# A two-layer token mixer on one core: the hand-written order of its calls on four engines is replaced by another order of the same calls

## The reference

```
x = x + layernorm(attn(layernorm(x)))
x = x + layernorm(ffn(layernorm(x)))

attn(h): conv = causal convolution of h over the sequence, kernel C * sigmoid(A)**t * B, plus D * h
         z = gelu(conv) @ W_proj.T + b_proj
         return layernorm(h + z) * gamma + beta
ffn(h):  r = sigmoid((mu_r*h + (1-mu_r)*h_prev) @ W_r.T)
         k = relu((mu_k*h + (1-mu_k)*h_prev) @ W_k.T) ** 2
         return r * (k @ W_v.T)
```

## Time and profile before

| What | Value |
|---|---|
| median of 3 runs | 150.51 us (150.22 to 150.79) |
| the profiled execution's own time | 150.25 us |
| its span, first to last instruction | 148.5 us |
| PE busy | 135.5 us (91%) |
| DVE, ACT, POOL busy | 130.8, 129.6, 127.5 us (88%, 87%, 86%) |
| DMA moved | 8.99 MB |
| chain that ended last | PE 73%, POOL 17%, DVE 4% |

### The profile page before, as it was taken

One profiled execution on the slowest core, in us unless ns is written; L12 is line 12 of the kernel. 1 busy time (PEld: TensorE's weight loads), 2 busy tenths in 40 slices (PEclk: granted clock), 3 DMA queues, 4 the chain that ended last, 5 costly groups with the idle time before them and its releaser, 6 DMA issues.

```text
span 148.5 us, 3239 instructions
## 1 busy us (share of the span) xinstructions
PE 135.5 (91%) x950; PEld 116.0 (78%) x950; DVE 130.8 (88%) x372; ACT 129.6 (87%) x388; POOL 127.5 (86%) x176
## 2 busy tenths in 40 slices
PE   6778888989999999999999999999999999999910
PEld 6667787876988799797979797988887887777900
DVE  0989999999999988999997999998999899339981
ACT  4878999799699999979779999959998988999940
POOL 4599999998989988989896998978999899978282
PEclk9999999999999999999999999999999999999995
DMA  3999900000000002000200002200200200424524
GB/s 89 235 328 272 299 22 0 0 2 0 0 4 0 0 0 77 0 2 0 75 0 0 0 4 71 73 0 7 71 2 0 71 4 0 141 68 138 152 72 141
DMA packets 18705, 8.99 MB, mean 61 GB/s; under 512 B 1536, under 2 KB 18688, under 8 KB 18688
## 3 DMA queue, kind: packets, MB, share of 16 engines
q1 hardware_dynamic: 17840, 8.52, 19.7%
q10 hardware_dynamic: 848, 0.26, 0.7%
HBM read 4.59 MB, written 4.19 MB: 59 GB/s over the span
## 4 chain that ended last, share of the span: by engine, by line
PE 73%; POOL 17%; DVE 4%; DMA 2%; issue 1%; POOLq 1%; ACT 0%
PE ps_k L855 9%; PE ps_k L856 9%; PE ps_r L867 9%; PE ps_r L866 9%; PE ps_tv L876 9%; PE ps_z L833 7%; POOL x_r L227 5%; POOL xn_pow L236 5%; PE ps_tv L846 5%; PE ps_prefix L813 4%; PE ps_z L834 4%; PE ps_xT L805 3%; PE ps_prefix L819 2%; PE ps_prefix L815 2%; DMA a_col<-in_A_param 2%
## 5 line engine op out<-in xcount | busy, mean ns | idle before, releaser
L370 ACT ACTIVATE xn<-x_all,x_bias,x_r 128x128 f32<-128x128 f32 x64 | 26.4, 499 | 1.1 <-POOL x_bias L218 0.6
L867 PE MATMUL ps_r<-mixed_T,tsT 128*128 128x128 f32 x128 | 24.7, 275 | 0.0
L866 PE MATMUL ps_r<-mixed_T,tsT 128*128 128x128 f32 x128 | 24.7, 275 | 0.0
L833 PE MATMUL ps_z<-pv_T,gelu 128*128 128x128 f32 x128 | 22.1, 275 | 0.0
L426 ACT ACTIVATE f_normal<-f,out_bias,yf_r 128x128 f32<-128x128 f32 x48 | 19.8, 493 | 1.5 <-POOL out_bias L285 1.5
L236 POOL TENSOR_TENSOR xn_pow<-xn,pow_token 128x512 f32<-128x512 f32 x16 | 20.3, 1273 | 0.0
L866 PEld LDWEIGHTS ps_r<-mixed_T,tsT 128*128 128x128 f32 x128 | 19.5, 192 | 0.5 <-issue 0.5
L833 PEld LDWEIGHTS ps_z<-pv_T,gelu 128*128 128x128 f32 x128 | 19.4, 191 | 0.5 <-issue 0.5
L389 ACT ACTIVATE junk<-ps_z 128x128 f32<-128x128 f32 x64 | 16.7, 280 | 3.2 <-PE ps_z L834 3.2
L867 PEld LDWEIGHTS ps_r<-mixed_T,tsT 128*128 128x128 f32 x128 | 19.4, 192 | 0.0
L834 PE MATMUL ps_z<-ident,xnT 128*128 128x128 f32 x64 | 17.4, 273 | 0.0
(11 more groups left out here) (112 smaller groups left out, 360.1 us busy)
## 6 DMA issues: line engine op xcount, KB each, us to landing
out_x<-x_all SPq DMA_DIRECT2D x15, 256.0 KB, 2.2
x_all<-in_x SPq DMA_DIRECT2D x7, 512.0 KB, 6.0
x_all<-in_x SPq DMA_DIRECT2D x2, 128.0 KB, 2.8
x_all<-in_x SPq DMA_DIRECT2D x1, 256.0 KB, 3.2
out_x<-x_all SPq DMA_DIRECT2D x1, 128.0 KB, 1.8
out_x<-x_all ACTq DMA_DIRECT2D x1, 128.0 KB, 1.9
w_pv<-in_W_proj ACTq DMA_DIRECT2D x1, 64.0 KB, 2.6
w_pv<-in_W_v ACTq DMA_DIRECT2D x1, 64.0 KB, 4.5
```

Source lines behind the costliest of these rows:

```text
L370: last = a_.activation(tile(xn[u % D], j), xa(u, j), ACT.Identity, bias=col(x_bias, u, j), scale=col(x_r, u, j))
L833: t_.matmul(tile(ps_z[u % 3], j), tile(gelu[u % D], j), pv_T[:, 0, :], start=True, stop=False)
L866: t_.matmul(tile(ps_r, j), tsT[u % D][:, q, l + 1:l + 1 + P], mixed_T[:, 0, :], start=True, stop=False)
L867: last = t_.matmul(tile(ps_r, j), tsT[u % D][:, q, l:l + P], mixed_T[:, 1, :], start=False, stop=True)
```

## The change

The four lists of calls are replaced by four other lists. Each engine still makes the same calls with the same arguments; no function, buffer, semaphore or transfer is different, and SP's list is not touched. Since the lists are a few lines shorter, the code of ACT and DVE stands 3 lines higher and that of PE 4. Of the lists themselves, which are rows of call names, one place is shown as it stands in the diff (the end of the DVE list):

```
-            add_f_late(11); add_fused(); subtract_y_mean(); gate(14)
-            f_stats_of(14); add_f_late(12); gate_half(0); f_stats_half(0); gate_half(1); f_stats_half(1)
-            centre_half(0); add_f_half(0); centre_half(1); add_f_half(1)
+            gate(14); f_stats_of(14); add_fused(); gate_half(0); gate_half(1); f_stats_half(0); f_stats_half(1)
+            centre_half(0); add_f_late(11); add_f_late(12); add_f_half(0); centre_half(1); add_f_half(1)
```

More of the change, by code:

```diff
@@ L741, in _ @@
[L741 to L755, removed]
@@ new lines, in _ @@
+            x_pooled(10, 2); residual(1); t_stats_of(1); convolve(5); gamma_z(2); gamma_z(3); scale_z(2); scale_z(3)
+            y_stats_of(2); y_stats_of(3); convolve(6); x_stats(12); residual(2); residual(3); t_stats_of(2)
+            t_stats_of(3); gamma_z(4); convolve(7); gate(0); f_stats_of(0); gamma_z(5); scale_z(4); scale_z(5)
+            y_stats_of(4); y_stats_of(5); convolve(8); gate(1); x_pooled(12, 2); residual(4); residual(5)
+            t_stats_of(4); t_stats_of(5); x_stats(14); f_stats_of(1); convolve(9); gamma_z(6); gamma_z(7); gate(2)
@@ L879, in values @@
                 last.then_inc(v_ready, 1)
-            centre_bias()
-            keep_busy(3); transpose_xn(0); keep_busy(6); prefix_sum(0); keep_busy(6); transpose_pv(); transpose_xn(1); prefix_sum(1)
-            project(0); transpose_xn(2); prefix_sum(2); project(1); transpose_xn(3); transpose_rk(); prefix_sum(3)
-            mix_weights(); transpose_xn(4); project(2); prefix_sum(4); project(3); transpose_xn(5); prefix_sum(5)
-            project(4); transpose_t(0); transpose_xn(6); prefix_sum(6); keys(0); gates(0); prefix_sum(7)
@@ L886, in _ @@
-            transpose_xn(7); transpose_t(1); project(5); values(0); keys(1); transpose_xn(8); project(6); gates(1)
-            transpose_t(2); prefix_sum(8); keys(2); values(1); gates(2); transpose_xn(9); transpose_t(3); project(7)
-            prefix_sum(9); values(2); keys(3); prefix_sum(10); transpose_xn(10); gates(3); transpose_t(4)
-            project(8); values(3); keys(4); transpose_xn(11); prefix_sum(11); project(9); transpose_t(5)
-            project(10); gates(4); transpose_xn(12); keys(5); values(4); prefix_sum(12); gates(5); transpose_t(6)
@@ L891, in _ @@
-            prefix_sum(13); keys(6); project(11); values(5); transpose_xn(13); gates(6); transpose_t(7)
-            prefix_sum(14); keys(7); transpose_xn(14); project(12); values(6); gates(7); prefix_sum(15)
-            transpose_t(8); project(13); keys(8); values(7); gates(8); transpose_xn(15); transpose_t(9); project(14)
-            values(8); keys(9); transpose_t(10); gates(9); project(15); values(9); keys(10); transpose_t(11)
-            gates(10); values(10); keys(11); transpose_t(12); gates(11); values(11); keys(12); transpose_t(13)
@@ L896, in _ @@
-            gates(12); values(12); keys(13); transpose_t(14); gates(13); values(13); keys(14); transpose_t(15)
-            gates(14); keys(15); values(14); gates(15); values(15)
+            centre_bias(); keep_busy(3); transpose_xn(0); keep_busy(6); prefix_sum(0); keep_busy(6); transpose_pv()
+            transpose_xn(1); prefix_sum(1); project(0); transpose_xn(2); prefix_sum(2); project(1); transpose_rk()
+            transpose_xn(3); prefix_sum(3); project(2); mix_weights(); prefix_sum(4); transpose_xn(4); project(3)
@@ new lines, in _ @@
+            transpose_xn(5); prefix_sum(5); project(4); transpose_t(0); prefix_sum(6); transpose_xn(6); gates(0)
+            keys(0); transpose_t(1); prefix_sum(7); transpose_xn(7); keys(1); project(5); values(0); project(6)
+            gates(1); transpose_t(2); prefix_sum(8); transpose_xn(8); values(1); keys(2); gates(2); transpose_t(3)
+            project(7); prefix_sum(9); transpose_xn(9); values(2); keys(3); prefix_sum(10); transpose_xn(10)
+            transpose_t(4); gates(3); keys(4); values(3); prefix_sum(11); transpose_xn(11); project(8); transpose_t(5)
@@ new lines, in _ @@
+            project(9); project(10); gates(4); values(4); prefix_sum(12); transpose_xn(12); keys(5); transpose_t(6)
+            gates(5); values(5); prefix_sum(13); transpose_xn(13); project(11); gates(6); keys(6); transpose_t(7)
+            transpose_xn(14); project(12); prefix_sum(14); values(6); keys(7); transpose_t(8); gates(7); project(13)
+            values(7); transpose_xn(15); keys(8); prefix_sum(15); transpose_t(9); project(14); gates(8); values(8)
+            keys(9); transpose_t(10); gates(9); project(15); values(9); keys(10); transpose_t(11); gates(10)
@@ L900 @@
+            values(10); keys(11); transpose_t(12); gates(11); values(11); keys(12); transpose_t(13); gates(12)
+            values(12); keys(13); transpose_t(14); gates(13); values(13); keys(14); transpose_t(15); gates(14)
+            values(14); keys(15); gates(15); values(15)
 _INS = ["x", "A_param", "B_vec", "C_vec", "D_vec", "W_proj", "b_proj", "gamma", "beta",
```

107 lines of the change are left out of this document (57 added, 50 removed).

## The result

The changed kernel takes 150.98 us (150.84 to 151.38, 10 runs) and the kernel before 150.47 us (150.22 to 150.79, 10 runs): a ratio of 1.0034, 95% interval 1.0023 to 1.0045. It is slower by 0.51 us, half of the 1.0 us that the prediction gave. The profiled executions differ by 0.67 us (150.92 and 150.25 us).

The account below looks back on a forecast made before the run. PE, busy without a break from 33.6 to 141.5 us, was taken to bound the kernel, with stores ending it. Start -0.1, full stretch +0.1, end +1.0 gave +1.0 us: 151.5 us on the median's scale, 8-in-10 range 149.8 to 152.6 us.

Parts of the forecast that it names:

- The end: Behind PE's last work: late additions of units 11 and 12 hold SP's stores, so the last lands later, +1.0 us.
- the start: Before 33.6 us: DVE's lost 0.76 us is given back and PE's full stretch begins earlier, -0.1 us.
- the bunch of stores: SP's end: stores of 11, 13, 12, unit 15's halves and 14, 1280 KB issued within 2.1 us from 143.87 us.
- The upper bound by the rate of loads: At the end: at the queued loads' 295 GB/s, 256 KB take 0.89 us and the end is 1.66 us later.
- the rival of stores that overlap: No change: stores overlap, or PE's earlier end pays for them; 0 at the end and on PE, 150.5 us; chance 0.22.
- It is then given back: On DVE: t_stats_of(0) moved behind convolve(4) returns 0.76 us, so convolve(4) and the sixth transposition stand where they stood.
- The swap on POOL: xn_pow ahead of a root: prefix_sum(5) loses its 0.46 us wait, but project(4) waits about 0.8 us for residual(1).
- The full stretch: From 33.6 to 141.5 us, PE always busy: later tanh_r(11) on ACT makes PE wait for values(12), +0.1 us.
- faster: PE's early convolution waits close by 1.5 us and stores cost only +0.5 us: 149.5 us; chance 0.15.
- clearly slower: DVE's 0.76 us at the start is not given back and stores pile up, +0.76 + 1.0: 152.3 us; chance 0.18.

Follow-up runs that it names:

- The same two calls moved in the kernel before: Kernel before with DVE's add_f_late(11) and add_f_late(12) moved between centre_half(0) and add_f_half(0): 151.53 us, ratio 1.0075 to the kernel before.
- Taking 256 KB out: Changed kernel with only SP's list edited, the store of unit 13 ahead of that of unit 11: 150.27 us, ratio 0.9990 to the kernel before.
- the start as before: Changed kernel with ACT's W_v load ahead of normalise(1), DVE's x_pooled(4,2) ahead of convolve(0), keep_pv ahead of x_pooled(6,2): 150.53 us, ratio 1.0011 to kernel before.
- the pair of statistics back: Changed kernel with x_pooled(4,2) back ahead of convolve(0) on DVE: 150.86 us, ratio 1.0026 to the kernel before.
- one swap: Kernel before with POOL's xn_times_pow(5) moved ahead of t_variance(0,1) and y_root(1,1): 150.84 us, ratio 1.0031 to the kernel before.

## Why the prediction was half right

The forecast was +1.0 us and +0.51 us was measured. The end held. The step that failed is the start: its term of -0.1 us was a loss of 0.64 us and gains of 1.0 us behind it, -0.36 us together. With it failed the assumption that PE ends where it did, and that the bunch of stores begins as late as the prediction has it.

*The end, +1.0 us: right.* The same two calls moved in the kernel before cost 1.1 us. The 1280 KB took the 3.8 us that the prediction worked out from 0.755 us for 256 KB, at the rate of the earlier trace rows. Taking 256 KB out gave back 0.7 us. The upper bound by the rate of loads was not needed, and the rival of stores that overlap is out. The Trainium skill, "DMA: Bandwidth & Descriptors", section "Specifications", has beside the fabric's figure that the prediction cited a limit of about 358 GB/s for a core's share of device memory; the 344 to 346 GB/s of the stores in the rows above lie 3 to 4% under that one. What sets their rate no run here shows.

*Where the bunch starts: 0.35 us too late.* "With the same end of PE the halves' first gate still begins at 141.42 us" failed. It began at 141.07 us: 0.25 us because PE was ahead, the rest because the gate no longer stood behind `add_f_late(12)`, which ended at 141.5 us before. The whole bunch moved with it, and its last bytes with the bunch.

*The start, -0.1 us: the term that was mis-sized, and its reasons were wrong.* DVE's wait ahead of the first convolution (0.68 us against 1.0), `keep_pv` (14.86 us against 15.0) and `project(0)` (15.39 against 15.5) came near where the prediction put them. But "It is then given back" failed: with the start as before PE ends 0.40 us earlier. The move of `t_stats_of(0)`, which was to give it back, is worth 0.25 us and not 0.7, and PE had caught up before DVE reached that call (at 29.05 us). PE's starts, from the rows above and the earlier trace rows, show where:

| PE begins | before, us | after, us | PE ahead by, us |
|---|---|---|---|
| `project(0)` | 14.91 | 15.39 | -0.48 |
| `project(1)` | 18.66 | 19.30 | -0.64 |
| `project(3)` | 27.48 | 27.56 | -0.08 |
| `prefix_sum(5)` | 30.39 | 29.75 | +0.64 |
| `project(4)` | 31.81 | 31.67 | +0.14 |
| the call behind `transpose_xn(6)` and `prefix_sum(6)` | 35.62 | 35.26 | +0.36 |
| the last `values` | 140.94 | 140.69 | +0.25 |

The new start puts PE 0.64 us behind. Between `project(1)` and `project(3)` it wins 0.56 us, where PE's own list has `transpose_rk` ahead of `transpose_xn(3)`, and `project(2)` and `prefix_sum(4)` ahead of `transpose_xn(4)`: the two waits of 0.41 us for a convolution are gone. The swap on POOL, booked as two waits of which one replaces the other, is about that: PE's lead grows by 0.72 us up to `prefix_sum(5)` and falls by 0.50 us at `project(4)`. `prefix_sum(6)` ahead of `transpose_xn(6)` goes with another 0.22 us. The prediction named PE's swaps and gave them no price. That they are the cause is read from the waits that went; no run takes them out alone.

*The full stretch, +0.1 us: the size came out, by luck.* From 35.3 us to its end PE's lead falls by 0.11 us. But ACT's `tanh_r(11)` began 0.55 us later than before, not 1.0 us, `values(12)` met no wait, and the lead is the same ahead of it and behind it. It falls by 0.20 us between 54.6 and 58.3 us, in gaps too small for the view of waits, and 0.10 us of that come back by 95 us.

*The sum.* By the profiled executions -0.25 + 0.9 = +0.65 us against 0.67 measured: -0.25 is PE's end, start and full stretch together, and 0.9 is the end's +1.0 less the 0.1 us that the gate came earlier on its own account. The remaining 0.16 us to the median's +0.51 lie in the scale: the profiled execution of before was 0.22 us under its median, that of after 0.06 us. Of the rivals, "faster" had the mechanism that made up for the start: PE's waits for a convolution went from 2.4 to 0.7 us, but its end came forward by only a sixth of the 1.5 us that this rival asked. The 0.76 us of "clearly slower" were lost at the start almost whole (0.64 us), and more than won back behind it.

## What to carry to other kernels

When an order changes behind the last matrix product, write down the queue of stores with its bytes: a call that costs nothing where it stands can release a queue, and the bytes behind it end the program when they run together. When two calls are swapped on one engine, follow the in-order lists of the engines that consume both, not only the two waits: here one swap cost 0.45 us in the old order, because of what stood behind it, and by PE's starts cost nothing in the new one. A cheap check is to look for idle time in which the moved call could have run; here it stood open for 1.55 us.

## What the runs showed that was not expected

SP's single issues took 0.37 us in the rows above, and the last two of the changed kernel's bunch, which follow the issue ahead of them at once, 0.57 and 0.50 us. From its issue to its landing the store of unit 14 took 2.2 us before and 3.0 us behind the others. The load of W_v, issued at the same place of the same list, made PE wait 0.32 us in the changed kernel's profiled execution and 0.86 us in that with the pair of statistics back. Yet the time did not change measurably when the load was put first: a wait that shows in a trace can stand wholly in the shadow of the next one.
